# A two-layer decoder kernel: the first attention projects its pairs of sequences eight ahead instead of six, and SyncE stores a pair's rows in the even body, behind that body's load

## The reference

```python
def _L0_attn_ref(x, W_attn, b_attn, W_proj, b_proj):
    B, T, C = x.shape          # 32, 128, 128
    H = N_HEADS                # 16
    D = C // H                 # 8
    qkv = x @ W_attn + b_attn
    q, k, v = jnp.split(qkv, 3, axis=-1)
    ...
    att = jnp.einsum('bhtd,bhsd->bhts', q, k) / jnp.sqrt(jnp.asarray(D, x.dtype))
    att = att + _alibi_causal_mask(T, H, x.dtype)[None]
    att = jax.nn.softmax(att, axis=-1)
    y = jnp.einsum('bhts,bhsd->bhtd', att, v)
    y = y.transpose(0, 2, 1, 3).reshape(B, T, C)
    return y @ W_proj + b_proj
...
x = x + _L0_attn_ref(_layernorm(x, axis=-1), L0_attn_W_attn, ...)
x = x + _L0_xattn_ref(ctx_1024, _layernorm(x, axis=-1), ...)
x = x + _L0_ffn_ref(_layernorm(x, axis=-1), ...)
x = x + _L1_attn_ref(_layernorm(x, axis=-1), ...)
x = x + _L1_xattn_ref(_layernorm(x, axis=-1), ctx_1024, ...)
x = x + _L1_ffn_ref(_layernorm(x, axis=-1), ...)
```

## Time and profile before

| | us |
|---|---|
| median of three runs | 2207.32 |
| lowest and highest | 2203.02, 2216.77 |
| the profiled execution's own time | 2224.03 |
| its span | 2222.1 |
| TensorE busy, share of the span | 2009.2, 90% |
| VectorE | 1559.2, 70% |
| ScalarE | 1365.8, 61% |
| GpSimd | 1017.7, 46% |
| chain that ended last, TensorE's share | 65% |

### The profile page before, as it was taken

How to read it: one execution, slowest core, us unless ns; L and a number is a source line. 1 busy time by engine, 2 the same in 40 slices (tenths; PEclk the granted TensorE clock), 3 DMA queues, 4 the chain that set the end, 5 groups by cost and what they waited for, 6 DMA issues and landing times.

```text
span 2222.1 us, 44461 instructions
## 1 busy us (share of the span) xinstructions
PE 2009.2 (90%) x14756; PEld 1706.2 (77%) x14817; DVE 1559.2 (70%) x3386; ACT 1365.8 (61%) x3150; POOL 1017.7 (46%) x1223
## 2 busy tenths in 40 slices
PE   4999989999999999998047999999879999999998
PEld 2777779999999999994045888778657777777776
DVE  4555658888888888777873666566567777777775
ACT  3656656666666666666764667777645555555554
POOL 2545444444445445420003655444335666566665
PEclk7999899999999999998577999999989999999999
DMA  5333600000000000000004344455323333343333
GB/s 151 117 112 94 151 10 1 1 1 1 2 1 1 2 1 1 1 1 1 0 1 128 112 115 114 119 150 144 90 88 121 126 119 120 114 125 119 121 126 95
DMA packets 138907, 161.01 MB, mean 72 GB/s; under 512 B 15341, under 2 KB 99245, under 8 KB 138285
## 3 DMA queue, kind: packets, MB, share of 16 engines
q1 hardware_dynamic: 137676, 157.79, 23.9%
q10 hardware_dynamic: 1008, 0.45, 0.1%
HBM read 119.75 MB, written 38.70 MB: 71 GB/s over the span
## 4 chain that ended last, share of the span: by engine, by line
PE 65%; issue 9%; POOL 8%; SPq 5%; ACT 5%; DVE 5%; DMA 3%; POOLq 0%; ACTq 0%; DVEq 0%
PE bank L836 7%; POOL h_lo L1952 7%; PE bank L250 5%; PE bank L800 5%; PE bank L802 5%; PE bank L801 5%; PE bank L1671 5%; PE bank L847 5%; PE bank L1673 4%; PE bank L1672 4%; PE bank L261 3%; PE bank L232 3%; SPq L642 2%; PE bank L1575 2%; PE bank L231 2%
## 5 line engine op out<-in xcount | busy, mean ns | idle before, releaser
L1952 POOL TENSOR_TENSOR h_lo<-h,h_hi 128x512 fp32r<-128x512 f32 x264 | 341.3, 1293 | 246.0 <-ACT h_hi L1772 245.8
L473 DVE TENSOR_REDUCE nmx<-bank 128x4 fp32r<-128x512 f32 (+1 forms) x384 | 238.1, 621 | 243.0 <-PE bank L232 240.1
L1201 POOL TENSOR_TENSOR pw<-ew,rw 128x410 f32<-128x410 f32 x256 | 225.9, 882 | 367.8 <-DVE rw L1060 362.2
L1765 ACT ACTIVATE sl<-bank 128x512 f32<-128x512 f32 x264 | 158.0, 599 | 238.5 <-PE bank L1673 235.9
L391 ACT ACTIVATE pt<-bank 128x512 f32<-128x512 f32 (+1 forms) x384 | 228.3, 599 | 118.2 <-PE bank L250 116.8
L956 ACT ACTIVATE ew<-bank,nmax 128x205 f32<-128x205 f32 x512 | 217.2, 432 | 132.3 <-DVE nmax L1052 132.3
L1893 DVE TENSOR_TENSOR bank<-bank,sl 128x512 f32<-128x512 f32 x264 | 184.1, 697 | 150.2 <-PE bank L1673 121.1
L600 POOL TENSOR_SCALAR_AFFINE_SELECT pt<-pt 128x512 f32<-128x512 f32 x256 | 162.5, 636 | 195.2 <-ACT pt L391 195.1
L250 PE MATMUL bank<-q_pack,k_diag 128*128 128x128 f32 (+1 forms) x1536 | 241.9, 282 | 3.4 <-ACT pt L391 3.1
L250 PEld LDWEIGHTS bank<-q_pack,k_diag 128*128 128x128 f32 (+1 forms) x1536 | 192.9, 184 | 52.2 <-issue 41.3
L836 PE MATMUL bank<-kvt,qs 128*128 128x205 f32 x1024 | 221.6, 339 | 0.0
(11 more groups left out here) (317 smaller groups left out, 5225.2 us busy)
## 6 DMA issues: line engine op xcount, KB each, us to landing
share_b<-share_rows SPq DMA_DIRECT2D x256, 256.0 KB, 3.2
q_rows<-q_hi SPq DMA_DIRECT2D x96, 128.0 KB, 2.9
q_pack<-q_rows SPq DMA_DIRECT2D x32, 384.0 KB
k_rows<-k_hi SPq DMA_DIRECT2D x64, 128.0 KB, 2.1
raw<-in_experts SPq DMA_DIRECT2D x33, 192.0 KB, 3.3
q_rows<-q_lo SPq DMA_DIRECT2D x48, 128.0 KB, 2.9
q_pack<-q_rows SPq DMA_DIRECT2D x32, 192.0 KB
k_diag<-k_rows SPq DMA_DIRECT2D x128, 48.0 KB
```

Source lines behind the costliest of these rows:

```text
L473: nc.vector.tensor_reduce(m.nmx[:, b % 2, :, 0, c], m.score[c % 2][:, 0:HC * a.columns].rearrange("p (h k) -> p h k", h=HC)[:, :, 0:a.keys ...
L1201: nc.gpsimd.tensor_tensor(m.pw[:, k, :, 0:KW], m.ew[:, k, :, :], m.rw[:, k, :].unsqueeze(2).broadcast_to([128, 2, KW]), ALU.mult)\
L1952: nc.gpsimd.tensor_tensor(m.h_lo[:, k % 3, :], m.h[:, (k + u) % 2, :], m.h_hi[:, k % 3, :].bitcast(F32), ALU.subtract).then_inc(s.los, 1)
```

## The change

The number of sequences that a front runs ahead becomes 8 for all three attentions, as a constant; so `attn0` has the fronts of four pairs in its prologue (0, 2, 4, 6) and those of twelve pairs in bodies 0 to 23. In `attn0` SyncE stores a pair (now b+6) in the even body, behind the load of sequence b+4. `save_queries` waits for the loads of the pair four before, for every pair and not for pair 4 alone. `attn1` and `cross` keep their order. `PE`, `DVE`, `ACT` and `POOL` only have the constant in place of the attribute; of these lines two stand here.

```diff
-        self.paired, self.ahead = paired, 8 if paired else 6
+        self.paired = paired
...
 SLOTS = 4
 RING = 3
+AHEAD = 8
...
     def body(b, u):
-        before, front = place(a, b - 1), place(a, b - u % 2 + a.ahead)
+        before, front = place(a, b - 1), place(a, b - u % 2 + AHEAD)
...
     if a.earlier is None:
-        for q in range(0, a.ahead, 2):
+        for q in range(0, AHEAD, 2):
             copy_inputs(a, q)
...
     def save_queries(a, q):
         v = q // 2 % 2
         wait(sp, a.s.query_lows, q + 2)
         if a.paired and q >= SLOTS:
             a.wait_loaded(sp, q - SLOTS)
-        elif q == SLOTS:
-            a.wait_loaded(sp, 0)
-            a.wait_loaded(sp, 1)
+        elif q >= SLOTS:
+            a.wait_loaded(sp, q - SLOTS)
+            a.wait_loaded(sp, q - SLOTS + 1)
...
     def by_sequences(b):
 
         if place(a, b + SLOTS):
             load_rows(*place(a, b + SLOTS))
-        if b % 2 == 1 and place(a, b - 1 + a.ahead):
-            save_queries(*place(a, b - 1 + a.ahead))
-            save_keys(*place(a, b - 1 + a.ahead))
+        if b % 2 == 0 and place(a, b - 2 + AHEAD):
+            save_queries(*place(a, b - 2 + AHEAD))
+            save_keys(*place(a, b - 2 + AHEAD))
```

More of the change, by code:

```diff
@@ L299, in body @@
             if c == 0 and u % 2 == 0 and front:
-                transpose_inputs(*front, (u + a.ahead) // 2 % 2, maxima_before)
+                transpose_inputs(*front, (u + AHEAD) // 2 % 2, maxima_before)
             if c == 0 and u % 2 == 1 and front:
@@ L314, in body @@
                 owner, n = place(a, b + 2)
-                done = b - u % 2 + a.ahead + 2 * (u % 2)
+                done = b - u % 2 + AHEAD + 2 * (u % 2)
                 transpose_maxima(owner, n, min(done, B) if isinstance(b, int) and a.later is None else done if owner is a else done - B)
@@ L337, in attention_tensor @@
         transpose_maxima(a, 1, 6)
-        for q in range(6, a.ahead, 2):
+        for q in range(6, AHEAD, 2):
             front(q, q // 2 % 2, 2)
@@ L410, in body @@
                 copy_maxima(*place(a, b + 1))
-            if c == 1 and a.later is not None and isinstance(b, int) and b == B - a.ahead - 4:
+            if c == 1 and a.later is not None and isinstance(b, int) and b == B - AHEAD - 4:
                 root_scalar(act, nc, m, m.s, 11, at=FIRST)
@@ L513, in body @@
                 context_statistics(b)
-            if c == 1 and a.later is not None and isinstance(b, int) and b == B - a.ahead - 4:
+            if c == 1 and a.later is not None and isinstance(b, int) and b == B - AHEAD - 4:
                 wait(dve, a.s.measured, B // 2)
                 variances(nc, m, m.s, link, m.stats, at=FIRST)
-            if c == 3 and a.later is not None and isinstance(b, int) and b == B - a.ahead - 4:
+            if c == 3 and a.later is not None and isinstance(b, int) and b == B - AHEAD - 4:
                 norms(nc, m, m.s, link, 11, m.stats, m.rstd, m.shift, at=FIRST)
@@ L525, in body @@
                 heads_out(*place(a, b - 1))
[L526 to L529, removed]
+            if c == 3 and u % 2 == 0 and place(a, b + AHEAD + 2):
+                normalise(*place(a, b + AHEAD + 2))
+            if c == 1 and u % 2 == 1 and place(a, b - 1 + AHEAD):
+                values(*place(a, b - 1 + AHEAD))
             if c < NC - 1 and place(a, b + 2):
@@ L611, in body @@
             tail(b)
-        if u % 2 == 1 and place(a, b - 1 + a.ahead):
-            query_lows(*place(a, b - 1 + a.ahead))
+        if u % 2 == 1 and place(a, b - 1 + AHEAD):
+            query_lows(*place(a, b - 1 + AHEAD))
         if a.causal:
             select(b, 2)
-        if u % 2 == 1 and place(a, b - 1 + a.ahead):
-            key_lows(*place(a, b - 1 + a.ahead))
+        if u % 2 == 1 and place(a, b - 1 + AHEAD):
+            key_lows(*place(a, b - 1 + AHEAD))
         if a.causal:
             select(b, 3)
-        if u % 2 == 1 and place(a, b + 1 + a.ahead):
-            add_base(*place(a, b + 1 + a.ahead))
+        if u % 2 == 1 and place(a, b + 1 + AHEAD):
+            add_base(*place(a, b + 1 + AHEAD))
         if a.split_weights:
@@ L632, in attention_pool @@
         widen_values(a, 0, 0)
-        add_base(a, a.ahead)
+        add_base(a, AHEAD)
     over_sequences(body)
@@ L684, in body @@
             load_more(b)
-        if a.later is not None and b == B - a.ahead - 4:
+        if a.later is not None and b == B - AHEAD - 4:
             sp.wait_ge(m.s.zeros, 10)
@@ L695, in by_sequences @@
             load_rows(*place(a, b + SLOTS))
-        if b % 2 == 1 and place(a, b - 1 + a.ahead):
-            save_queries(*place(a, b - 1 + a.ahead))
-            save_keys(*place(a, b - 1 + a.ahead))
+        if b % 2 == 0 and place(a, b - 2 + AHEAD):
+            save_queries(*place(a, b - 2 + AHEAD))
+            save_keys(*place(a, b - 2 + AHEAD))
     def by_pairs(b):
[L702 to L706, removed]
+        if b % 2 == 1 and place(a, b + AHEAD + 1) and place(a, b + AHEAD + 1)[0].cross:
+            load_context(place(a, b + AHEAD + 1)[1])
+        if b % 2 == 0 and place(a, b - 2 + AHEAD):
+            save_queries(*place(a, b - 2 + AHEAD))
+            save_keys(*place(a, b - 2 + AHEAD))
         if b % 2 == 1 and place(a, b + 2 * RING - 1):
```

## The result

The changed kernel takes 2302.79 us (median of 4 runs, 2297.25 to 2310.71); the kernel before, run beside it on the same chip, 2208.01 us (4 runs, 2203.02 to 2216.77). The ratio is 1.0412, with a 95% interval of 1.038 to 1.0443: 94.8 us slower. The prediction was 2297.2 us. The profiled execution of the changed kernel took 2302.41 us, that of the one before 2224.03, which makes 78.4 us between the two profiles.

What follows compares the result with a forecast made beforehand. TensorE was taken as the bound, at 13.63 us a pair of bodies. Stalls 56.4 + clock 43.2 - loss 16.7 + prologue 4.2 + late landings 2.8 = +89.9 us on the median 2207.32 gave 2297.2 us, range 2250 to 2337.

Steps and rivals of the forecast that it cites:

- What goes: attn0 bodies 1 to 23: loads no longer wait for stores, so k_diag stalls and their low clock go, 16.7 us less.
- The stall: Odd bodies: q_lo waits for stores behind a load, landed 9.17 us after scores_t; TensorE stalls 4.7 us, 12 times, 56.4 us.
- Late landings: Stores of the bodies: every landing is now on the path, 2.8 us added, bounds 0 and 8.
- The clock: TensorE behind each stall: low clock costs 3.6 us, 12 times, 43.2 us; bounds 0 and 5.8 a stall.
- The prologue: Before body 0: first exponentials 5.9 us later, at 58.2, as q_lo of pair 6 waits for stores; net +4.2 us.
- the front that goes: TensorE in the bodies: a pair of bodies loses its front, some 1.7 us of work, set against the prologue's 5.9.
- the first (clock hardly falls): Rival 1, TensorE in the bodies: stalls come but the clock hardly falls, 2254.0 us; chance 0.20.
- the second: Rival 2, TensorE: clock stays low up to each pair's next t = 0, 2323.6 us; chance 0.22 together with rival 4.
- the third: Rival 3, SyncE's even body: stores land early enough, q_lo isn't late, only the freed loads count, 2194.8 us; chance 0.05.
- the fourth: Rival 4, SyncE: its new wait for the slots' loads holds the stores, some 2315 us; chance 0.22 together with rival 2.

Runs made afterwards that it cites:

- (1): The changed kernel with SyncE's even body turned round, the pair's stores issued ahead of the load: 2219.54 us, ratio 1.0054 to the kernel before.
- experiment 8: The changed kernel with a second set of q_lo, q_hi, k_lo, k_hi in the first attention, SyncE's order untouched: 2203.78 us, ratio 0.9949 to the kernel before.
- experiment 6: The changed kernel with only q_pack's DMA of the load ahead of the stores, the four of k_diag behind them: 2252.85 us, ratio 1.0207.
- experiment 4: The changed kernel with 20 unused matmuls put into TensorE's stall in the odd bodies: 2269.4 us, ratio 1.0282 to the kernel before.
- experiment 2: The changed kernel with three row buffers and the stores in the odd body, still eight ahead: 2210.95 us, ratio 1.0016 to the kernel before.
- experiment 5: The kernel before once more, the whole change undone: 2207.57 us, ratio 1.0005; its profiled execution took 2195.04 us.

## Why the prediction was right

The mechanism is shown from four sides: the order of SyncE (1), the buffer (8), a part of the load (6), the clock (4). By the steps of the prediction:

- **What goes.** The stalls on `k_diag` went. Eight ahead with landed loads, a pair took 13.59 to 13.64 us (2, 8), the undisturbed value of the earlier trace rows. But the 16.7 us belonged to that one execution; another one of the same kernel had 4.6 (5). The forecast had named this: with less of the loss at the median "less goes". It took the 16.7 off the median too, and that was the wrong choice, some 12 us.
- **The stall.** Predicted 4.7 us a pair, 12 times; it was 5.0, 59.5 us for 56.4. From the load's start to `q_lo` the twelve pairs needed 9.29 to 10.41 us, mean 9.77, for 9.17.
- **Late landings.** 12 x 0.60 = 7.2 us more on ScalarE, of which TensorE's stalls show 59.5 - 56.4 = 3.1; the term had 2.8. The size was right and the cause wrong: they were not landings. From the last issue to `q_lo` it was 2.2 us in all pairs but one (2.48); late was, in the main, SyncE's issuing, as in the 2.17 us above.
- **The clock.** Predicted 3.6 us a pair between 0 and 5.8; it was 21.57 - 13.63 - 5.0 = 2.9, and experiment 4 gives 29 to 33 us for all. This is the mis-sized term of the sum: 43.2 for 34.8. The price was near the 2.8 us worked out from the earlier trace rows, not the 4.3 of the earlier trace rows. The mean over 75 to 300 us was 0.81, as predicted 0.7 to 0.9. By the rule of the Trainium skill (TensorE: Matmul & The Clock Gate, "HAM oscillation") the fall is paid at every such wait, and the trace agrees: 0.50 behind the stall shown, the alibi matmul at 0.65 us instead of 0.39 behind each of the twelve, and 2.9 us a pair on the mean. With the shorter stalls of experiment 6 it was paid at nine of twelve.
- **The prologue.** Predicted 5.9 gross; body 1's `q_lo`, its own hold set aside, came at 71.46 - 3.60 = 67.86, 4.9 late. The working was right too: the first exponentials came at 58.02 for 58.2, 5.7 us later than before (52.31), and of that 0.8 was made up by `q_lo` of body 1. The low clock in body 0 is not the cause, since the kernel before had it as well (experiment 2). In experiment 8 the exponentials come at 55.85, because `q_lo` waits 2.16 us for TensorE's keys instead of 4 for the stores, and the clock rises at about 56 us, so that body 0 takes 6.9 us instead of 9.8: body 1's `q_lo` comes at 62.71, no later than before. Why the clock rises sooner there isn't shown. No run isolates the 1.7 us for the front that goes.

Against the two profiles: 59.5 + 34.8 (12 x 2.9) + 4.9 - 1.7 (the front that goes) - 16.7 = 80.8 us, for 78.4 measured. Against the medians the loss counts with some 4.6: 92.9 for 94.8. The forecast's +89.9 lies 3.0 below that 92.9, and this is the sum of its errors: the clock 8.4 too large, the prologue 1.0 too large, stalls with late landings 0.3 too small, and the loss 12.1 too large. The two large ones cancelled in part, which was luck; that the time came within 0.3% speaks for the mechanism more than for each term. How large the loss is in a median run stays open: two profiles of the kernel before had 16.7 and 4.6 us, and the medians of experiments 2 and 8, whose pairs are undisturbed, point to between 0 and 8 us. That is an estimate: body 1's `q_lo` came 5.2 us later but the median was only 4.4 slower (2), and 0.3 us earlier but the median 7.8 faster (8); the 1.7 us would lower both differences.

Of the rivals, the first (clock hardly falls) is refuted by 0.50 behind the stall and by experiment 4; the second by the clock that is back before the next t = 0 in the pair shown, and by 21.57 us a pair instead of 24; the third by the 12 waits; the fourth by SyncE's first store, issued 0.11 us after the load's last DMA: it waited for nothing.

## What to carry to other kernels

When a transfer is moved behind an item of its queue that waits for the computation, ask who waits for the transfer's source to come free, not only who needs what it brings: that waiter's own queue carries the delay on, here over an exponential and a select to TensorE. Such a wait on a reused buffer is cheap to break with a second buffer, and then the order that had cost 4% gave 0.5%. And price a repeated stall of TensorE by more than its length: here 5.0 us of stall cost 2.9 us of clock on top.

## What the runs showed of the hardware

- TensorE's clock fell behind stalls well under 5 us: behind nine of twelve stalls of 1.4 to 3.5 us, and with them it averaged 0.83 to 0.96 over stretches of 30 us (experiment 6). Stalls of 1.41, 1.43 and 1.53 us left it up, another of 1.43 did not.
- The low clock in body 0 costs 3 to 4 us: from the first exponentials to `q_lo` of body 1 it took 10.3 us, most of it at 0.50 (experiment 2), and 6.9 us at 1.00 (experiment 8).
- The granted clock in a trace can be wrong. In experiment 5 it is 1.00 up to 61 us, while four matmuls take the 1.12 us that they take at 1.2 GHz (0.66 at 2.4). The duration of a known instruction is the test.
- An fp32 matmul of 128 columns with its own load of weights took 0.226 us here at a granted clock of 1.00, two records each (7.23 / 32).
- SyncE issues one of these DMAs in 0.6 us as a rule, but in 6 of the 12 pairs of the changed kernel the eleven issues together took 0.5 to 1.2 us longer than the 7.02 of the earlier trace rows. The cause is open.
- From body 23's `q_lo` to the end, two executions of the same kernel differed by 17 us (1992.5 and 1975.4).
